# Two message-passing layers of a four-layer graph kernel: rows normalised in place, and another order of work on four engines

## What is computed

```python
x = _layernorm(x + _L0_gnn_ref(x, adj, ...))   # attention over neighbours
x = _layernorm(x + _L1_gnn_ref(x, adj, ...))   # GATv2, 8 heads
x = _layernorm(x + _L2_gnn_ref(x, adj, ...))   # MLP on pairs of nodes
x = _layernorm(x + _L3_gnn_ref(x, adj, ...))   # graph convolution

def _layernorm(x, axis=-1, eps=1e-05):
    m = jnp.mean(x, axis=axis, keepdims=True)
    v = jnp.var(x, axis=axis, keepdims=True)
    return (x - m) / jnp.sqrt(v + eps)

# L1: masked softmax over neighbours of attention scores, then a weighted sum
g_sum = g_r[:, :, None, :, :] + g_l[:, None, :, :, :]
e = jnp.einsum('bijhf,f->bijh', jax.nn.leaky_relu(g_sum, SLOPE), w_attn)
e = jnp.where(mask == 0, -jnp.inf, e * mask)
a = jax.nn.softmax(e, axis=2)
out = jax.nn.leaky_relu(jnp.einsum('bijh,bjhf->bihf', a, g_r), SLOPE)

# L2: an MLP and a layer norm on every pair, then a sum weighted with adj
h = jax.nn.relu(hi[:, :, None, :] + hj[:, None, :, :] + b1)
y = jnp.einsum('bijk,kl->bijl', h, W2) + b2
y = _layernorm(y, gamma, beta)
out = jnp.einsum('bij,bijh->bih', adj, y)
```

## Time and profile before

| | |
|---|---|
| median of three runs | 1641.01 us |
| the profiled execution, its own time | 1644.35 us |
| its span, first to last instruction | 1642.6 us |
| TensorE matmul busy | 1403.2 us (85%), 9038 instructions |
| VectorE busy | 1289.9 us (79%), 2530 |
| ScalarE busy | 1025.6 us (62%), 2743 |
| GpSimd busy | 5.4 us, 24 |
| TensorE's mean granted clock | 0.942 of 2.4 GHz |

### The profile page before, as it was taken

How to read it: one execution, slowest core, us unless ns; L and a number is a source line. 1 busy time by engine, 2 the same in 40 slices (tenths; PEclk the granted TensorE clock), 3 DMA queues, 4 the chain that set the end, 5 groups by cost and what they waited for, 6 DMA issues and landing times. The chain is left out here.

```text
span 1642.6 us, 28358 instructions
## 1 busy us (share of the span) xinstructions
PE 1403.2 (85%) x9038; PEld 1183.1 (72%) x9081; DVE 1289.9 (79%) x2530; ACT 1025.6 (62%) x2743; POOL 5.4 (0%) x24
## 2 busy tenths in 40 slices
PE   3665688899999999999999985999999999995664
PEld 2554466787887878788787884888788888884664
DVE  4887578676886868878687654899899999897788
ACT  2564678655656656656565213878878788785554
POOL 1000000000000000000000000000000000000000
PEclk9997799999999999999999997999999999998777
DMA  2220466787786868768687675977777777770222
GB/s 72 65 64 26 163 264 255 273 311 271 278 307 254 297 253 311 295 253 304 254 301 264 232 242 199 338 258 263 263 254 268 250 259 268 252 248 17 71 64 71
DMA packets 137587, 367.62 MB, mean 224 GB/s; under 512 B 12897, under 2 KB 71905, under 8 KB 137441
## 3 DMA queue, kind: packets, MB, share of 16 engines
q1 hardware_dynamic: 137040, 365.81, 62.7%
q10 hardware_dynamic: 400, 0.00, 0.0%
HBM read 231.54 MB, written 134.22 MB: 223 GB/s over the span
## 5 line engine op out<-in xcount | busy, mean ns | idle before, releaser
L1060 PE MATMUL wide<-W2c,c_h 128*128 128x128 f32 x1280 | 174.3, 275 | 9.7 <-ACT c_h L1112 6.1
L659 PE MATMUL wide<-b_vv,put_w 128*128 128x512 f32 (+1 forms) x384 | 170.7, 526 | 12.8 <-DVE b_vv L836 10.9
L836 DVE TENSOR_TENSOR b_vv<-duo,b_vv 128x512 f32<-128x512 f32 (+1 forms) x192 | 113.7, 600 | 85.8 <-ACT b_vv L757 85.7
L887 DVE TENSOR_TENSOR b_wt<-bank,b_aT 128x512 f32<-128x512 f32 (+1 forms) x192 | 109.2, 598 | 88.7 <-PE bank L701 82.4
L685 PE MATMUL bank<-b_wt,b_SITl 128*128 128x136 f32 x1280 | 169.7, 290 | 8.7 <-DVE b_wt L887 8.7
L685 PEld LDWEIGHTS bank<-b_wt,b_SITl 128*128 128x128 f32 x1280 | 164.1, 199 | 16.5 <-DVE b_wt L887 11.2
L1060 PEld LDWEIGHTS wide<-W2c,c_h 128*128 128x128 f32 x1280 | 170.6, 194 | 3.4
L1130 ACT CAST c_zz<-c_z 128x512 fp32r<-128x512 f32 (+1 forms) x192 | 105.0, 547 | 96.4 <-DVE c_z L1201 96.4
L701 PE MATMUL bank<-b_grl,b_SJl 128*128 128x128 f32 x1280 | 155.9, 277 | 1.7 <-ACT b_aT L764 1.7
L701 PEld LDWEIGHTS bank<-b_grl,b_SJl 128*128 128x128 f32 x1280 | 150.4, 194 | 2.2 <-issue 2.0
L1208 DVE TENSOR_TENSOR c_zz<-c_z,c_zz 128x512 fp32r<-128x512 f32 (+1 forms) x192 | 114.9, 599 | 26.7 <-ACT c_zz L1130 23.5
(11 more groups left out here) (217 smaller groups left out, 3174.6 us busy)
## 6 DMA issues: line engine op xcount, KB each, us to landing
si_d<-b_SI SPq DMA_DIRECT2D x64, 640.0 KB, 2.9
sj_d<-b_SJ SPq DMA_DIRECT2D x64, 640.0 KB, 4.1
sit_d<-b_SIT SPq DMA_DIRECT2D x64, 640.0 KB, 5.3
b_SJl<-sj_d SPq DMA_DIRECT2D x64, 640.0 KB, 5.7
b_SITl<-sit_d SPq DMA_DIRECT2D x64, 640.0 KB, 5.9
c_SJ<-sj_d SPq DMA_DIRECT2D x64, 640.0 KB, 5.2
c_SI<-si_d SPq DMA_DIRECT2D x64, 640.0 KB, 6.5
c_SIT<-sit_d SPq DMA_DIRECT2D x64, 640.0 KB, 4.0
```

The source lines that it names most:

```text
L659: pe.matmul(out, e.put_w[:, pos, :], vv[:, (pos + k) % 2, 0:width(k)], start=(pos == 0), stop=False)
L836: v.tensor_tensor(vv[:, b, 0:w], bU[b][:, 0:w], vv[:, b, 0:w], ALU.max).then_inc(v_ok, 1)
L887: v.tensor_tensor(wt[:, mb, 4 * k:4 * k + rr, 0:P].rearrange("p r (h f) -> p r h f", h=HEADS), ring[k][:, 0:P * rr].rearrange("p (r h f) - ...
L1060: d = pe.matmul(bY[k][:, a:a + P], h[:, k, a:a + P], e.W2c[:, :], start=False, stop=(j == last))
```

## The change

In both layers `normalise_x` scales the rows of a graph in place in `cur` and waits for nothing; the buffer `xin` is gone, the transposes read `cur`, and VectorE no longer scales the old rows before it adds them (L433 and L1263 fall away). `centre` does the division by 128 and the subtraction in one instruction (L443 and L1234 fall away).

Layer 1: the exponential moves from the end of the step to the place before the copy of `xT`. The squares move there too, from steps n mod 4 = 1 to n mod 4 = 3, two steps later. The copies to `aT` come after the copy out of the sums. On TensorE the T step runs both gathers and the sum O first, then transposes the exponentials, then `score(0)`, then S.

Layer 2: ScalarE takes `keep_high` later in three places, VectorE takes `keep_low` one chunk later (chunks 0, 1, 2 of graph n - 1 in step n in place of 1 and 2 of n - 1 and 0 of n), `bb` is made by GpSimd in 64 instructions of 128x128, and the mean is taken in the step of the subtraction.

```diff
-def normalise_x(act, e, s, K, pos, late):
+def normalise_x(act, e, s, K, pos):
     n = 8 * K + pos
-    if late:
-        act.wait_ge(s.xT_mm, n - 1)
-    act.activation(s.xin[:, pos % 2, :], e.cur[:, bass.ds(n, 1), :].rearrange("p a f -> p (a f)"), ACT.Copy,
-                   scale=e.rstd[:, bass.ds(n, 1)]).then_inc(s.x_ok, 1)
+    act.activation(e.cur[:, n, :], e.cur[:, n, :], ACT.Copy, scale=e.rstd[:, n:n + 1]).then_inc(s.x_ok, 1)
...
 def centre(v, e, s, z, i):
     z.add(v.tensor_reduce(s.mean[:, :], s.res[:, :, :], AX.X, ALU.add))
     z.wait()
-    z.add(v.tensor_scalar(s.mean[:, :], s.mean[:, :], 1.0 / P, None, ALU.mult))
-    z.wait()
-    v.tensor_tensor(e.cur[:, bass.ds(Q * i, Q), :], s.res[:, :, :], s.mean[:, :].unsqueeze(2).broadcast_to([P, Q, P]),
-                    ALU.subtract).then_inc(s.cen_ok, 1)
+    v.scalar_tensor_tensor(e.cur[:, Q * i:Q * i + Q, :], s.mean[:, :].unsqueeze(2).broadcast_to([P, Q, P]), -1.0 / P,
+                           s.res[:, :, :], ALU.mult, ALU.add).then_inc(s.cen_ok, 1)
...
+        def spread(n):
+            return n % Q == 3 and n >= LAG + 9
...
                         gather(0)
-                    if T:
-                        pe.wait_ge(ex_ok, K)
-                        if A:
-                            pe.wait_ge(s.sit_ok, 3 * n + 3)
-                        if inner or m > 0:
-                            pe.wait_ge(w_ok, 3 * m)
                     if A:
                         gather(1)
-                    if T:
-                        transpose_exponentials(ring[2], 0)
-                        transpose_exponentials(ring[0], 1)
                     if O:
...
                     if A:
                         pe.wait_ge(s.sit_ok, 3 * n + 3)
+                    if T:
+                        pe.wait_ge(ex_ok, K)
+                        if m > 0:
+                            pe.wait_ge(w_ok, 3 * m)
+                        transpose_exponentials(ring[2], 0)
+                        transpose_exponentials(ring[0], 1)
+                        if A:
+                            score(0)
                     if S:
...
             @block.scalar
                     if A:
                         slope(0)
-                    if soft(n, 6):
-                        keep_exponentials(ring[2], 0)
                     if A:
                         slope(1)
-                    if soft(n, 6):
-                        keep_exponentials(ring[0], 1)
...
                         act.copy(os[:, (o // Q) % 2, o % Q, :], ring[1][:, 0:W]).then_inc(os_ok, 1)
+                    if soft(n, 6):
+                        keep_exponentials(ring[2], 0)
+                        keep_exponentials(ring[0], 1)
...
                         shorten_rows(act, s, K, pos + 1, inner or g >= 1)
+                    if soft(n, 5):
+                        act.wait_ge(z_ok, K)
+                        act.activation(top[:, :], top[:, :], ACT.Exp).then_inc(ex_ok, 1)
+                    if spread(n):
+                        squares(act, e, s, fours(n) - 1, range(Q))
+                    if N:
                         act.wait_ge(s.xT_mm, g + 1)
...
-                    if soft(n, 5):
-                        act.wait_ge(z_ok, K)
-                        act.activation(top[:, :], top[:, :], ACT.Exp).then_inc(ex_ok, 1)
-                    if centred(n):
-                        squares(act, e, s, fours(n), range(Q))
...
             @block.gpsimd
+                for m in range(B):
+                    if m >= Q:
+                        pool.wait_ge(seq_c, 4 * (m // Q) - 2)
+                    pool.tensor_scalar(bb[:, m % Q, :], e.bet[:, :], e.deg[:, 0, m:m + 1], None,
+                                       ALU.mult).then_inc(bb_ok, 1)
...
             @block.vector
                     if F:
                         total(n - 1, 2)
-                        keep_low(n - 1, (pos - 1) % 2, 1)
+                        keep_low(n - 1, (pos - 1) % 2, 0)
...
-                        keep_low(n - 1, (pos - 1) % 2, 2)
+                        keep_low(n - 1, (pos - 1) % 2, 1)
...
                         total(n, 1)
-                        keep_low(n, pos % 2, 0)
+                    if F:
+                        keep_low(n - 1, (pos - 1) % 2, 2)
```

More of the change, by code:

```diff
@@ L566, in finished @@
         def finished(n):
-            return n % Q == 3 and n >= LAG + 5
+            return n % Q == 3 and LAG + 5 <= n <= B + LAG + 1
         def joined(n):
@@ L703, in step @@
                             d.then_inc(g_mm, 1)
-                    if A:
-                        if pos == 0 and (inner or n > 0):
+                    if A and not T:
+                        if pos == 0 and n > 0:
                             pe.wait_ge(es_ok, K)
@@ L901, in step @@
                     if joined(n):
-                        f = Steps(v, seq_c, 7 * fours(n))
+                        f = Steps(v, seq_c, 5 * fours(n))
                         f.n = 3
                         f.wait()
-                        residual(v, e, s, f, fours(n))
+                        own = e.cur[:, Q * fours(n):Q * fours(n) + Q, :]
+                        f.add(v.tensor_tensor(s.res[:, :, :], s.res[:, :, :], own, ALU.add))
                     if centred(n):
-                        f = Steps(v, seq_c, 7 * fours(n))
-                        f.n = 5
+                        f = Steps(v, seq_c, 5 * fours(n))
+                        f.n = 4
+                        f.wait()
                         centre(v, e, s, f, fours(n))
@@ L921, in step @@
                         select_rows(v, e, s, K, pos + 2, inner or n + 2 >= 4)
[L923 removed]
+                every_step(v, step, LAG + 6)
 def layer2_packed(nc, e):
@@ L981, in layer2_packed @@
         o_read = sem("o_read")
+        bb_ok = sem("bb_ok")
         seq_c = sem("seq_c")
@@ L1144, in step @@
                         root(n - 1, 2)
+                        keep_high(n - 1, (pos - 1) % 2, 1)
                     if A:
@@ L1174, in step @@
                         root(n, 1)
+                        keep_high(n, pos % 2, 0)
                 every_step(act, step, 7, 2)
@@ L1227, in step @@
                     if part(n, pos, inner, 3):
[L1228 removed]
+                        q.n = 2
                         q.wait()
[L1230 to L1234 removed]
+                        q.add(v.tensor_tensor(s.res[:, :, :], s.res[:, :, :], e.cur[:, Q * i:Q * i + Q, :], ALU.add))
                     if F:
```

61 lines of the change are left out of this document (16 added, 45 removed).

## The result

The changed kernel takes **1575.95 us** (median of four runs, 1573.45 to 1576.21), beside 1641.03 us for the kernel before on the same chip: a ratio of 0.960, 95% interval [0.958, 0.962]. The forecast was 1576 us.

The account below looks back on a forecast made before the run. TensorE was taken to bound layer 1, with layer 2 nearly as full on TensorE and VectorE. Gains of 39 (layer 1), 25 (layer 2's steps) and 1 us (its end) make 65, so 1641 becomes 1576 us, range 1559 to 1594.

Parts of the forecast that it names:

- steps 1 and 2 of the T step: Layer 1's T step: 2.67 us of idle TensorE before the second gather, then 3.1 us lost at slow clock.
- The first T step: Layer 1, n = 14: 3 us gain, bounds 0 and 5, as the exponential's table load may return as a wait.
- The end of layer 1: Last batch of layer 1: VectorE operations that fall away form a chain there, 0.9 us gained.
- the steps n mod 8 = 1: Layer 1: squares moved away free the SIT copies, but two gathers cover them; gain 0, at most 1 us.
- Layer 2's four steps: Layer 2, four steps from 30.46 to 28.6 us: 1.86 gained, 25 us over 54 steps, bounds 11 and 40.
- the lower end: Layer 2: the loss of 2.97 us per four steps shrinks only in proportion to VectorE's batch work, 0.8 us gained.
- The wait of the sum for the late low: Layer 2, n mod 4 = 1: TensorE's sum L1077 waits 0.5 to 0.6 us for the last keep_low, now behind total.
- the floor of 27.49: Layer 2: four steps near its start, without batch work, where TensorE shows hardly a gap; 6.87 us a step.
- The stated reason: Layer 2: ScalarE no longer waits at keep_high for VectorE while rectify, which TensorE's MLP needs, is ready; gain above the proportion.
- The bound from above: GpSimd rival, chance 0.02: each of 64 tiles holds VectorE 0.69 us, 44 us in all, giving 1620 us.
- The end of layer 2: VectorE's chain at layer 2's end: 1.5 us fall away, later lows give back some 0.5, 1 us gained.
- The range: Whole kernel: 1559, layer 2 near its floor, to 1594, both layers at their lower ends, computed as 1641 - 36 - 11.

Follow-up runs that it names:

- squares-last run: Layer 2's two ScalarE squares instructions moved to the end of the step, behind keep_high(n, 0), against the changed kernel: 1567.79 us, ratio 0.9546.

## Why the prediction was right, point by point

*The wait in front of the second gather and the slow clock behind it* (steps 1 and 2 of the T step): right, and shown. The wait and the clock of 0.5 to 0.6 come and go together in the run with both orders undone, and with neither the T step is 12.48 us (forecast 12.4). 34.4 us were measured for six steps, 35.1 forecast. What the prediction did not see is that the two reorderings do the same thing: it argued with ScalarE's places, and TensorE's order would have given 29 of the 39 us by itself.

*The first T step*: mis-sized. It gained 5.35 us, above the taken 3 and the bound of 5. I had let about 2 us of the table load (1.28 us, at 292.57) come back as a wait. In the trace the copy of xT is late by that (295.04, 2 us after its transpose), but TensorE has other work by then: the projection's weight load waits 0.77 us for it, and the granted clock stays at 1.00 through the 11.44 us of the step.

*The end of layer 1*: 0.9 forecast, 1.8 measured; the steps n mod 8 = 1 gave 0.6 where 0 was taken with a bound of 1. Layer 1 in all 42.0 in the profiles, forecast 39, bounds 33 and 42.

*Layer 2's four steps*: 28.91 us, forecast 28.6, so 1.55 us gained per four and not 1.86; over 54 steps 21.5 us and not 25. The pieces: the load was worth 0.8, as the lower end had it. The wait of the sum for the late low is where I put it, 0.27 us and not 0.5 to 0.6, but 0.33 in front of the transpose ahead of it also counts, where 0.2 was taken. The rest is what was mis-sized: 28.91 us are 1.42 over the floor of 27.49, the two waits are 0.60 of that, and 0.82 remain where I allowed 0.4. The stated reason holds for the kernel before and was one half too many: ScalarE's wait in front of keep_high does hold up rectify and the MLP (0.84 us in the run with the old order), but it is cured by VectorE's later keep_low, which makes z come earlier. Moving keep_high brought nothing on top of that.

*GpSimd*: the forecast cost of nothing holds for the time, but not the picture of two engines that leave each other alone. A tile takes 0.60 us, three times the memset that I bounded it with from below, and 1.47 beside two operations of VectorE with two SBUF inputs; a batch's four are done in 3.2 of 28.9 us, and 25 us of idle time stand in front of them. So the contention is there, and in the changed kernel GpSimd waits and not VectorE. The bound from above (one tile holds VectorE for 0.69 us or more) is excluded: with five times the tiles no keep_low grew by more than 0.12 us.

*The end of layer 2*: 1 us forecast, 5.8 measured. From the last sum to `rstd` it is 2.3 us less: some 1.4 by the operations that fell away, which I had at 1.5, and 0.9 because the last sum runs 1.61 us and not 2.50, at a granted clock of 0.85 and not 0.50. Those 0.9 are chance: TensorE idles 1.87 us in front of this sum and not 4.85, but behind 1.88 us of idle time the same kernel's other profile has 2.10 us (0.62), the squares-last run 2.50 us (0.50) behind 1.55, and the run with layer 2's old order 1.79 us (0.75) behind 4.18. The other 3.5 us lie between the last transpose and the last sum (28.76 to 25.24 us). The runs take these apart: with layer 2's old order the stretch is 27.70 us, and with only ScalarE's keep_high in the old places 25.15. So 1.1 us came with the load and 2.5 with VectorE's later keep_low. The step that failed is that I had costed the end as if it were a part of the steady steps, against which the late lows "give back". Where an order is changed, the drain of a pipeline is priced by its whole chain.

*The range*: its upper end of 1594 used 36 us for layer 1, while the bound worked out for that layer was 33; by its own terms it is 1641 - 33 - 11 = 1597.

The sum: against its 65 us, the 54 steps brought 3.5 us less and the T steps 0.7 less, the end of layer 2 brought 4.8 more, layer 1's other terms 3.9 more (2.35 + 0.9 + 0.6), and the first nine steps vary by 1.5. That makes 71 us between the profiles, of which 5.8 are not in the medians, since one profile stood above its median and the other below. So the hit within 0.1 us is partly luck; single terms were off by up to 5 us, with both signs.

## What to carry to other kernels

Idle time of TensorE costs more than itself when the clock falls behind it: 2.67 us of waiting cost another 3.1 here, while 1.04 us left the clock alone in the same place. When a change undoes one wait in two ways, undo each alone and both together before crediting either. And where two engines hand halves of a job to each other, putting the dependent half one piece later (keep_low behind the next total) takes the waits off both, and what then pays is to keep everything that nobody waits for, like the sums of squares, behind what the next step's first matmul needs. Before saying that two engines do not disturb each other, look at single instructions and not at the mean of a group: here one tile in four took 1.47 us and the others 0.60.

## What was not expected of the hardware

- The first nine steps of layer 2 took 54.1 to 57.1 us in profiles whose code differs there by little or nothing. The granted clock goes with it: its mean over these steps is 0.92 in the two shortest (54.14 and 54.25 us), 0.91 in the changed kernel (54.75) and 0.89 in the longest (57.13) and in the kernel before (56.28). In the changed kernel it is 0.50 for the first 9.82 us of them. Other stretches of equal code repeat closely (the end of layer 1 took 104.5 to 105.1 us in twelve of the thirteen profiles of the changed kernel and its variants).
- A `tensor_scalar` of 128x128 fp32 takes GpSimd 0.60 us, and 1.47 beside two operations of VectorE with two SBUF inputs; a memset of that size takes 0.21. The other way round, a keep_low beside a GpSimd tile took up to 0.80 us and not 0.68.
- The last sum of layer 2 took 1.61 to 2.50 us behind 1.87 to 1.88 us of idle TensorE, in profiles that have the same work there, at a granted clock of 0.85 down to 0.50. A gain or loss of 0.9 us at this place says nothing of a change.
